# Moving the softmax normalization of each head pair earlier in the issue order of an attention plus mixture-of-experts kernel

## The reference

```
xn = layernorm(x)
Q, K, V = xn @ Wq + bq, xn @ Wk + bk, xn @ Wv + bv        # 16 heads of 16
attn = softmax(Q K^T / 4 + alibi)                          # per batch and head, 1024 x 1024
a = (attn @ V) @ Wo + bo
w = top-2 softmax gates of xn @ Wg over 8 experts
m = sum_e w_e * (silu(xn W1_e) * (xn W2_e)) W3_e + (silu(xn Ws1) * (xn Ws2)) Ws3
out = x + a + m
```

## Time and profile before

| | |
|---|---|
| median of 3 runs | 2625.7 us (2624.27 to 2627.22) |
| the profiled execution | 2625.7 us, span in the trace 2623.9 us |
| TensorE busy | 2506.3 us (96% of the span) |
| VectorE busy | 2114.8 us (81%) |
| ScalarE busy | 1687.1 us (64%) |
| GpSimd busy | 858.6 us (33%) |
| mean granted TensorE clock | 0.975 of 2.4 GHz |

### The profile page before, as it was taken

The page is one execution under the profiler, slowest core; times in us unless marked ns, Lnnn a source line. Parts: engine busy times, 40 slices in busy tenths (PEclk is TensorE's granted clock), DMA queues, the critical chain, the costliest instruction groups (busy, mean ns, idle before and its releaser), DMA issues.

```text
span 2623.9 us, 51186 instructions
## 1 busy us (share of the span) xinstructions
PE 2506.3 (96%) x20186; PEld 1553.1 (59%) x20186; DVE 2114.8 (81%) x3518; ACT 1687.1 (64%) x2314; POOL 858.6 (33%) x920
## 2 busy tenths in 40 slices
PE   4999999999999999999999998999999999999998
PEld 3775333333333333333333333999999988788887
DVE  7886999999999998998999992777777755555554
ACT  2444777888788887877888886777777742222222
POOL 4333454101101015554520101433343434433333
PEclk8997999999999999999999997999999999999999
DMA  5996555322222224444432213777777744433332
GB/s 181 339 327 219 185 199 191 85 65 74 71 68 81 72 85 142 148 147 132 141 96 69 65 56 110 250 234 244 237 241 240 239 134 111 107 99 97 97 97 81
DMA packets 213391, 384.15 MB, mean 146 GB/s; under 512 B 45264, under 2 KB 134544, under 8 KB 203792
## 3 DMA queue, kind: packets, MB, share of 16 engines
q1 hardware_dynamic: 175040, 218.25, 27.1%
q0 software_dynamic: 37024, 161.83, 19.4%
q10 hardware_dynamic: 1088, 0.79, 0.1%
HBM read 248.84 MB, written 141.43 MB: 149 GB/s over the span
## 4 chain that ended last, share of the span: by engine, by line
PE 77%; DVE 11%; DMA 4%; ACT 3%; issue 3%; POOL 1%; SPq 0%; POOLq 0%; ACTq 0%; DVEq 0%
PE ps L477 75%; DVE OPS L1092 3%; DVE mx L921 2%; PE ps L490 2%; DVE VB L1089 2%; ACT OPS L848 1%; DMA xr<-Xn 1%; DMA OPS<-mT 1%; POOL Xs L1231 1%; DVE OL L1078 1%; ACT OPS L830 1%; DVE VB L1109 0%; DVE xn L895 0%; DMA vst<-Vd 0%; DMA xt<-in_x 0%
## 5 line engine op out<-in xcount | busy, mean ns | idle before, releaser
L921 DVE TENSOR_REDUCE mx<-ps 128x1 f32<-128x512 f32 x2048 | 1270.8, 684 | 71.4 <-PE ps L477 67.0
L477 PE MATMUL ps<-OPS 54*128 54x512 f32 (+1 forms) x4096 | 831.0, 464 | 17.1 <-DMA OPS<-mT 10.4
L477 PEld LDWEIGHTS ps<-OPS 52*128 52x128 f32 (+1 forms) x4096 | 352.9, 188 | 514.3 <-issue 426.2
L776 ACT ACTIVATE pta<-ps 128x1024 f32<-128x1024 f32 x512 | 524.7, 1025 | 157.5 <-PE ps L477 151.6
L776 ACT ACTIVATE ptb<-ps 128x1024 f32<-128x1024 f32 x512 | 525.9, 1028 | 138.4 <-PE ps L477 132.8
L477 PE MATMUL ps<-OPS,WB 128*128 128x256 f32 (+1 forms) x2268 | 363.3, 312 | 3.3 <-DVE WB L1043 1.8
L477 PE MATMUL ps<-ptb,VB 128*32 128x256 f32 x4096 | 336.8, 402 | 0.0
L477 PE MATMUL ps<-pta,VB 128*32 128x256 f32 x4096 | 336.3, 401 | 0.2
L477 PEld LDWEIGHTS ps<-OPS,WB 128*128 128x128 f32 x2268 | 310.4, 180 | 32.8 <-issue 3.9
L477 PE MATMUL ps<-OPS,WB0c 128*128 128x256 f32 (+3 forms) x1440 | 256.6, 329 | 1.0 <-ACT accs L783 1.0
L1195 POOL TENSOR_TENSOR accs<-accs,asum 128x512 f32<-128x512 f32 x64 | 81.9, 1280 | 533.6 <-DMA asum<-Sd 533.5
(11 more groups left out here) (154 smaller groups left out, 2929.3 us busy)
## 6 DMA issues: line engine op xcount, KB each, us to landing
OPS<-QKh SPq DMA_DIRECT2D x512, 64.0 KB
Xs<-zero POOLq DMA_DIRECT2D x71, 256.0 KB, 4.7
xr<-Xs SPq DMA_DIRECT2D x71, 256.0 KB, 5.3
Ys<-VB SPq DMA_DIRECT2D x71, 256.0 KB, 5.0
QKh<-qkH SPq DMA_DIRECT2D x16, 1024.0 KB, 7.0
QKl<-qkL SPq DMA_DIRECT2D x16, 1024.0 KB, 8.3
OPS<-QKl SPq DMA_DIRECT2D x256, 64.0 KB
asum<-Sd SPq DMA_DIRECT2D x64, 256.0 KB
```

Of the source, the lines that this page charges most:

```text
L477: return self.e.matmul(o, l, r, start=start, stop=stop)
L776: self.e.activation(pt(n), ps[:, b:b + 2, :], ACT.Exp).then_inc(sem["exp"], 1)
L921: e.reduce_max(mx[:, k2, hh, i, half:half + 1], ps[:, bank, :], AX.X).then_inc(sem["mxred"], 1)
```

## The change

The four steps of `heads` for pair r - 1 are put one even call apart, all in pair r: i = 0 at kc = 0, i = 1 at kc = 2, i = 2 at kc = 4, i = 3 at kc = 6. Within kc = 0, the step i = 0 now comes behind the first two of the four calls of `load_pair` rather than ahead of all. For the last pair, whose steps lie among the first blocks, steps 1 to 3 come behind the three up-projections of block 0, each a call or more earlier.

```diff
         self.block_up(0, 0)
+        self.heads(NPAIR - 1, 1)
         self.split_block(1, 0)
...
             self.block_up(b, 1)
             if b == 0:
-                self.heads(NPAIR - 1, 1)
+                self.heads(NPAIR - 1, 2)
             if b:
                 self.block_down(b - 1)
...
             self.block_up(b, 2)
-            if b < 2:
-                self.heads(NPAIR - 1, b + 2)
+            if b == 0:
+                self.heads(NPAIR - 1, 3)
             if b + 3 <= NBLK + 1:
                 self.gather_weights(b + 3)
...
             if kc == 0:
                 self.next_pair(r)
-            elif kc >= 4 and r >= 1:
-                self.heads(r - 1, kc // 2 - 1)
+            elif r >= 1:
+                self.heads(r - 1, kc // 2)
...
     def next_pair(self, r):
-        if r >= 1:
-            self.heads(r - 1, 0)
         for i in range(4):
+            if i == 2 and r >= 1:
+                self.heads(r - 1, 0)
             if 1 <= r and r + 3 < NPAIR:
                 self.load_pair(r + 3, i)
-        if r >= 2:
-            self.heads(r - 2, 3)
```

## The result

The changed kernel takes 2673.3 us (median of 4 runs, 2671.45 to 2677.4) where the kernel before takes 2626.5 (4 runs, 2624.27 to 2628.9): a ratio of 1.018, 95% interval 1.0163 to 1.0198, 47 us slower. The forecast was 2620.5 us with a range of 2609 to 2634.

The account below looks back on a forecast made before the run. TensorE was taken to bound the pair loop and block stage, VectorE close behind. End -8.7, block start +1.5, early pairs -2 and scatter stage +4 sum to -5.2 us: 2625.7 to 2620.5 us, range 2609 to 2634.

Parts of the forecast that it names:

- Its own sign of being wrong: Whole kernel: wrong if VectorE's waits on `sq` exceed 10 us, or if the end of attention doesn't move.
- Between them I take -2: Early pairs 1 to 8, reciprocal two chunks earlier: -2 us net, between bounds of -9 and +27.
- rival B: Early pairs: `sq` lands over 3.0 us after issue in most, stopping VectorE; +13.5 us, 2636 us in all; chance 0.14.
- only a part of the burst is ahead: Early pairs: only part of GpSimd's clears and packing precedes `sq`; a reason for taking -2 us.
- I take +4: Scatter stage: multiply ahead of the last two scatters makes `xr` and `mneg` later; +4 us, bounds 0 and 15 pairs x 1 us.
- The loop itself (`mneg` to `mneg`) is under 20.5 us, so a quiet pair loses nothing: Scatter stage: GpSimd's loop fits the pair's 20.5 us; only `xr` landing after 6 us, not 4.8, stops TensorE.
- Its sum is unchanged: Four scatter-stage pairs that also load V: GpSimd's queue has no wait on `asum`, so the existing TensorE stop stays unchanged.
- Rival C: Scatter stage: GpSimd becomes the bound, each of 15 pairs a microsecond longer; +15 us, 2631.5 us in all; chance 0.12.
- -8.7: End of attention: `mT` issued before the weight gathers removes a 6 us stop; 8.7 us gained, bounds 0 and 15.7.
- +1.5: Start of the blocks: slot load and weight gather stand behind pair 63's multiply; 1.5 us lost, between 0 and 3.5.
- rival A: End of attention: clock kept in pair 63, gain 15.7 us; 2615 us in all; chance 0.18.
- That costs nothing in a quiet stage: Quiet pairs: `sq` has 3.0 us left until the reciprocal's new place, against 1.9 needed, so no cost.

Follow-up runs that it names:

- h3: Kernel before with the reciprocal alone moved from kc = 4 to kc = 2: 2620.4 us, ratio 0.9984, before at 2626.0.
- h1: Changed kernel with multiply and store back at kc = 0 of the pair after: 2622.3 us, ratio 0.999, before at 2626.0.
- f3: Changed kernel with the reciprocal put back from kc = 2 to kc = 4: 2655.8 us, ratio 1.0112, before at 2623.6.
- g4: Changed kernel with the `xr` load one call ahead of the multiply, nothing else: 2697.8 us, ratio 0.9962, before at 2705.9.
- f1: The changed kernel itself, run again on another chip beside the kernel before: 2663.7 us, ratio 1.0143.
- h4: Changed kernel with reciprocal back at kc = 4 and `xr` load at kc = 6 of the pair before: 2599.9 us, ratio 0.9898, before at 2626.0.
- e1: Changed kernel with the reciprocal put back from kc = 2 to kc = 4: 2661.9 us, ratio 0.9895, before at 2693.5.
- g2: Changed kernel with reciprocal back at kc = 4 and `xr` load at kc = 6 of the pair before: 2680.8 us, ratio 0.9892, before at 2705.9.
- e2: Changed kernel with the denominator copy put back ahead of all four loads: 2648.6 us, ratio 0.983, before at 2693.5.
- i2: i1 with all four steps also one even call apart in pair 62: 2585.1 us, ratio 0.9858, before at 2623.8.
- f4: Kernel before with only the multiply of pair 61 moved ahead of the weight gathers: 2613.3 us, ratio 0.9964.
- i1: h2 with the reciprocal at kc = 2 in pairs 1 to 9 alone: 2587.7 us, ratio 0.9878, before at 2623.8.
- h2: Kernel before with pair 61's multiply ahead of the gathers and `xr` load one call pair earlier: 2595.7 us, ratio 0.9889, before at 2626.0.
- e4: Kernel before with only the multiply of pair 61 moved ahead of the weight gathers: 2684.7 us, ratio 0.9969, before at 2693.5.
- g3: Kernel before with pair 61's multiply ahead of the gathers and `xr` load one call pair earlier: 2670.8 us, ratio 0.9881, before at 2705.9.
- e3: Kernel before with the reciprocal alone moved from kc = 4 to kc = 2: 2697.8 us, ratio 1.0003.
- g1: Changed kernel with multiply and store back at kc = 0 of the pair after: 2680.2 us, ratio 0.9914, before at 2705.9.

## Why the prediction was wrong

Wrong in sign and size. Two of its terms failed, both of the kind "a stop that might come"; the terms on what the change removes held. Its own sign of being wrong, waits on `sq` of over 10 us, is met: 13.0 us in the early pairs and 25.4 in the scatter stage.

**"Between them I take -2" (early pairs): +29.5 measured.** This is the largest error together with the next. The mechanism was the prediction's own, rival B: `sq` behind GpSimd's burst, landing in 6.4 us as `mT` had the earlier trace rows, stopping VectorE. It was priced at up to 3.4 us in 8 pairs; measured were 1.37 to 2.91 us in 6 pairs, 13.0 in all, yet the stage lost more than the bound of 27. What the bound left out is what it had itself read for `mT`: after a stop TensorE runs slower for a while (0.58 from 331 to 343 in the earlier trace rows; 0.51 and 0.61 over the 8 us behind the stops at 301.5 and 329.5 here). Of the 29.5 us, 11.7 are TensorE standing longer and 17.9 the same matmuls at a lower clock (windows above), so a wait of VectorE of 2.2 us in the mean cost nearly 5. The reason for taking -2, "only a part of the burst is ahead", is refuted: that part is enough, with the early reciprocal. It takes both. The reciprocal alone (h3), it and the copy without the multiply (h1), and the multiply with a late reciprocal (f3) leave 198 to 201 us; all of them make 225 to 234 (g4, f1 and the changed kernel). h4 at 209.8 lies between, with two waits on `sq`, 5.4 us, and one stop of TensorE of 2.80 us, behind which the granted clock is 0.50 for 8 us. In these pairs h4 has the same order as e1, f3 and g2, which take 201.3, 200.3 and 203.3, so this is scatter between executions or chips. Why one `sq` lands after 6.3 us and another in time behind a burst of about the same size is open.

The rule cited there, of the Trainium skill (DMA: Bandwidth & Descriptors, Queues, rings and completion order), is that each DMA engine takes turns between queues with work. It gives no landing time; that `sq` would then land in some 2 us was the prediction's reading. The 6.3 us at 321.57 speak against that reading for a small transfer behind a burst, as the row at 1578.38 did.

**"I take +4" (multiply inside the scatter stage): +37.4 measured, +29.8 on the second chip.** The failing step is "The loop itself (`mneg` to `mneg`) is under 20.5 us, so a quiet pair loses nothing". By the prediction's own terms the loop is 20.4 us: 21.9 from the end of one `mneg` (+7.0) to the next (+8.4 of the next pair), less the slack of 1.5. The mis-sized term in it is the landing of `xr`, taken as 4.8 us; with the change it is 5.6 to 7.5 with a median of 6.3, which puts the loop over 20.5 in every pair. `asum` at 5.7 held (5.4 in f3 and in the changed kernel). The distance between two `mneg` measures 21.9 us in f3 and 22.2 in the changed kernel. There the late queue reaches TensorE by another way, for which the prediction had no term in this stage: GpSimd late at the multiply, the `OTd` store late, `sq` behind it and half of the loads, VectorE stopped. That the two steps feed each other was not seen: that `sq` leaves at "+1.9 of the next pair" was worked out for a quiet pair, but with the V load it was +5.5 (1028.47 to 1033.99); and the 1.9 us for its landing were 4.1 to 5.5 us in each of the 14 pairs that waited. In the quiet pairs 50 to 59 `sq` leaves 1.3 to 2.0 us behind the copy, as forecast, and no reciprocal waits. "Its sum is unchanged", for the four pairs that also load V, looked at GpSimd's queue alone, not at SyncE's behind it. That both go through the `xr` wait is shown for the stops for `mneg` (f3 against h4, on two chips where the kernel before takes 2623.6 and 2626.0). For the waits on `sq` it rests on g4, where none is left, on a chip on which the changed kernel itself wasn't run. Rival C named the place; its price of 1 us per pair was less than half of the 2.3 measured (37.4 / 16), again for want of the clock (30.2 of the 37.4 us are matmuls at the lower clock). That the loss needs the multiply's move is shown by h1; that the copy's place has a share in it is likely (e2), not shown.

**"-8.7" (end) and "+1.5" (start of the blocks): -12.3 and +0.1 measured, -16.0 and +1.5 on the second chip.** Right in each step: `mT` ahead of the gathers, no stop there, gathers right behind the multiply, a wait of ScalarE for the weights (1.28 us for the 1.5 forecast; landed 6.5 us after issue for 6.2). Forecast and rival A both occur: 40.4 us in this execution, with a granted 0.56 from 1670 to 1682, and 35.3 in f1 and 35.2 in i2, with the clock kept (52.7 - 35.3 = 17.4 for A's 15.7). Alone (f4) it is worth 10.4 us. The size of ScalarE's wait for `WR0c` goes with the level: 0.96 to 1.18 us where the clock was kept (g4, i2, f1), 1.28 here and 1.74 in e2 (40.9 us), 4.03 to 4.60 in f4, i1 and h2, which took 42.9 to 44.4 us.

**"That costs nothing in a quiet stage" (reciprocal):** nearly. Pairs 9 to 33 take 504.0 to 504.3 us in each of the eight profiled executions with the reciprocal at kc = 2 there (h3 has it alone) and 501.7 to 502.0 in the others: 2.3 us over 24 pairs. No view shows a wait for it; where in VectorE's queue it arises is open.

**The clock rule of the Trainium skill** (TensorE: Matmul & The Clock Gate, What's actually happening) is that activity releases the throttle. Here from 329 to 337 the clock is at 0.58 and from 337 to 345 at 1.00, with TensorE busy: this trace agrees with it in the early pairs. The prediction doubted it for pair 63 by the earlier trace rows, and no run says why that pair stayed low for 28 us.

## What to carry to other kernels

When a step is moved up in a queue that also carries other engines' inputs, write down the loop from one of its outputs to the next, with every landing at its slowest row, and compare it with the period: here two landings of 5 to 6 us in one loop filled a period of 20.5 us, and taking one of them out (issue the load a call earlier) was worth more than the change was meant to bring. Price a stop of an engine that is 98% busy by the stop and the clock behind it, not by the stop alone. Two moves that are each harmless in a stage may be harmful together, as the early reciprocal and the early multiply in pairs 0 to 9, so cost them as a pair where one delays what the other waits for.

## What the runs showed of the hardware

**Chips differ in one stage.** The kernel e4 takes 425.5 us for pairs 33 to 49 on one chip, and as f4 350.5 on another, while the other stages agree within 6 us. So do g3 and h2 (410.8, 328.3). On those two chips several engines sometimes stop at the same time, for what the trace only calls remote. Timeline of e4 in that stage:

```profile
1029.22 2.48 DVE L923 TENSOR_REDUCE mx<-ps 128x1 f32<-128x512 f32 x4 [3.32 <-remote]
1029.32 1.94 ACT L778 ACTIVATE ptb<-ps 128x1024 f32<-128x1024 f32 x2 [3.26 <-PE ps L479]
...
1029.97 0.79 PE L479 MATMUL ps<-OPS 52*128 52x512 f32 x1 [2.05 <-DVE mx L923]
```

VectorE and ScalarE stop together for 3.3 us, TensorE for 2.05. Such rows are in six of the eight traces from these chips, 8 to 18 of them where the multiply is at kc = 0 (e3, e4, g1, g3) and up to 2 where it is at kc = 6, and in none of the twelve from others. They aren't the whole difference: g4 has none and still takes 396.5 us, and g2 has two and takes 413.6 us where h4, the same kernel, takes 328.5. So an order can look better or worse by its chip: the late reciprocal is 1.1% faster than the kernel before in e1 and 1.1% slower in f3, with the same stage time of its own (395.8 and 393.7 us). The cause is open.

**Runs of one order** differ by 5 to 10 us in pairs 0 to 9 (198.4 and 203.7 for g3 and h2; 203.3 and 209.8 for g2 and h4). The six profiled executions with the reciprocal at kc = 2 and the multiply at kc = 0 there (e3, g1, h1, h3, i1, i2) lie at 197.3 to 198.8, so i1's gain of some 4 us in these pairs over the order of before (198.0 to 204.6 in its six) is likely, not shown.
